# Layer 1 of a two-layer model: smaller pieces of the expert work, deeper buffers, and the expert sum moved to ACT and GpSimd

## The reference

```python
# per batch b (8), T = 512 tokens, C = 128, H = 16 heads of 8
bias attention (a = 0): softmax(q k^T / sqrt(8) + bias[h, j - i]) v, then a gate and a residual
h = affine(layernorm(x));  h = h + causal attention(a = 1) of rmsnorm(h), through Wo
t = rmsnorm(h);  logits = t @ gate_w                          # 8 experts, top 2, gates by softmax
hid = silu(einsum('td,edh->teh', t, w1))                      # 8 experts, 256 wide, all computed
ye = einsum('teh,ehd->ted', hid, w2)
h = h + einsum('te,ted->td', combine, ye);  out = x + gate * h
```

## Time and profile before

| what | us |
|---|---|
| time, median of 3 runs | 2226.02 (2208.1 to 2226.34) |
| time of the profiled execution | 2220.59 |
| its span | 2218.9 |
| busy PE, DVE, ACT, POOL | 1844.8, 1467.2, 1039.1, 807.5 |
| mean granted TensorE clock | 0.923 of full speed |
| first instruction of layer 1 | 778.9 |
| first and last attention tile of layer 1 on DVE | 822.3, 2128.7 |

### The profile page before, as it was taken

One profiled execution on the slowest core, in us unless ns is written; L12 is line 12 of the kernel. 1 busy time (PEld: TensorE's weight loads), 2 busy tenths in 40 slices (PEclk: granted clock), 3 DMA queues, 4 the chain that ended last, 5 costly groups with the idle time before them and its releaser, 6 DMA issues.

```text
span 2218.9 us, 56873 instructions
## 1 busy us (share of the span) xinstructions
PE 1844.8 (83%) x21312; PEld 1333.9 (60%) x21312; DVE 1467.2 (66%) x4551; ACT 1039.1 (47%) x2022; POOL 807.5 (36%) x1180
## 2 busy tenths in 40 slices
PE   3289989898936627998999999999999999999986
PEld 1167767777724415665666666666666666666654
DVE  5477787887720026686776776876876877867754
ACT  2045545544513214555654554654654554654531
POOL 0100110100030035666654654654654654654510
PEclk7589999999968858999999999999999999999988
DMA  3222221211024221112012012012012012011111
GB/s 138 67 84 66 71 63 57 58 51 41 7 81 141 66 83 36 47 35 80 14 67 80 25 67 81 25 64 83 24 62 80 29 62 77 27 62 48 64 37 33
DMA packets 89270, 132.18 MB, mean 60 GB/s; under 512 B 7834, under 2 KB 73754, under 8 KB 87339
## 3 DMA queue, kind: packets, MB, share of 16 engines
q1 hardware_dynamic: 54828, 98.31, 13.3%
q10 hardware_dynamic: 30848, 18.88, 2.9%
q0 software_dynamic: 3328, 11.40, 1.6%
HBM read 98.48 MB, written 30.23 MB: 58 GB/s over the span
## 4 chain that ended last, share of the span: by engine, by line
PE 43%; issue 7%; DVE 5%; DMA 4%; POOL 2%; ACT 2%; SPq 1%; ACTq 0%; POOLq 0%; DVEq 0%
PE ps L1553 14%; PE ps L1566 8%; PE ps L1539 6%; PE ps L1642 5%; PE ps L1636 5%; DMA l_stack<-parts_dram 3%; DVE l_X L1694 2%; PE ps L1576 1%; POOL l_Y L1407 1%; PE ps L1597 1%; ACT PT L1447 1%; DMA parts_dram<-l_parts 1%; PE ps L1586 1%; POOL y L1392 1%; PE ps L1606 1%
## 5 line engine op out<-in xcount | busy, mean ns | idle before, releaser
L1407 POOL TENSOR_SCALAR l_Y<-l_X,l_nmax 128x512 f32<-128x512 f32 (+3 forms) x1024 | 671.2, 657 | 576.4 <-PE ps L1553 327.3
L1447 ACT ACTIVATE PT<-ps 128x512 f32<-128x512 f32 (+3 forms) x1024 | 521.6, 518 | 488.3 <-PE ps L1553 414.1
L1553 PE MATMUL ps<-ident,l_Y 128*128 128x128 f32 x3328 | 563.4, 284 | 56.5 <-POOL l_Y L1407 35.8
L1553 PEld LDWEIGHTS ps<-ident,l_Y 128*128 128x128 f32 x3328 | 389.3, 144 | 263.1 <-issue 136.1
L1694 DVE CUSTOM_DVE_ANT_0 l_X<-ps,strips 128x512 f32<-128x512 f32 x512 | 351.1, 689 | 148.1 <-PE ps L1539 116.6
L1539 PE MATMUL ps<-l_stack 72*128 72x512 bf16 (+3 forms) x1024 | 357.5, 351 | 56.8 <-DVE l_nmax L1694 32.4
L1694 DVE CUSTOM_DVE_ANT_0 l_X<-ps,mask 128x384 f32<-128x384 f32 (+3 forms) x512 | 246.0, 488 | 134.5 <-PE ps L1539 92.2
L1566 PE MATMUL ps<-PT,v_aug 128*32 128x128 f32 x6656 | 236.9, 278 | 0.0
L1566 PEld LDWEIGHTS ps<-PT,v_aug 128*32 128x32 f32 x6656 | 166.9, 110 | 74.6 <-ACT PT L1447 44.8
L1539 PEld LDWEIGHTS ps<-l_stack 72*128 72x128 bf16 x1024 | 105.0, 103 | 89.4 <-DVE l_nmax L1694 46.2
L1642 PE MATMUL ps<-l_w_e,l_hid 128*128 128x128 f32 x1024 | 136.6, 290 | 15.7 <-DVE l_hid L1876 15.7
(11 more groups left out here) (279 smaller groups left out, 2596.3 us busy)
## 6 DMA issues: line engine op xcount, KB each, us to landing
stack<-parts_dram SPq DMA_DIRECT2D x48, 432.0 KB
l_stack<-parts_dram SPq DMA_DIRECT2D x64, 288.0 KB
l_stack<-parts_dram SPq DMA_DIRECT2D x192, 96.0 KB
l_w_e<-in_L_ffn_w_dram ACTq DMA_DIRECT2D x128, 128.0 KB, 2.4
parts_dram<-l_parts SPq DMA_DIRECT2D x32, 384.0 KB, 2.6
strips<-bias_dram POOLq DMA_DIRECT2D x16, 448.0 KB, 11.8
parts_dram<-parts SPq DMA_DIRECT2D x16, 432.0 KB, 2.6
w_e<-in_L_ffn_w_dram SPq DMA_DIRECT2D x16, 256.0 KB, 4.9
```

Of the source, the lines that this page charges most:

```text
L1407: nc.gpsimd.tensor_scalar(Y[:, n % Y_BUFS, 0:w], X[:, n % X_BUFS, 0:w], -1.0, nmax[:, n % 8:n % 8 + 1], ALU.mult, ALU.add).then_inc(y_pool, 1)
L1447: nc.scalar.activation(dst, src, ACT.Exp).then_inc(moved, 1)
L1553: last = nc.tensor.transpose(ps[:, to, k * P:(k + 1) * P], Y[:, n % Y_BUFS, k * P:(k + 1) * P], ident[:])
```

## The change

1. Expert outputs: two halves (`HALVES`) of two token tiles each, in banks 6 and 7. ACT copies each tile from PSUM with its gate as scale into `piece` (which is `xf`), four copies for an expert; GpSimd adds `piece` to `h_tok`, two adds of 128x256. DVE's four additions go.
2. The steps: hidden products two steps apart, output halves two steps apart and later, the whole batch 6 steps earlier in its stage; the last batch has a table of its own (`LAST_STAGES`) with two steps per expert, and its hidden products use banks 0 to 2.
3. Buffers: X 3, Y 4, `hid` 2, expert weights 3. `T_LAG` = 3: a tile is turned, moved and used one step later than before.
4. POOL's gather is issued as one DMA at each of steps 40, 44, 48 and 52.
5. `v_aug` has 10 columns per head in place of 32; bank 5 is cleared once by DVE at the start.

```diff
-MOE_START = {b: TILES * PLACE[1, b + 1] for b in range(B - 2)}
-MOE_START[B - 2] = TILES * PLACE[1, B - 1] + 18
-MOE_START[B - 1] = MOE_START[B - 2] + TILES
-STEPS = MOE_START[B - 1] + TILES
...
-X_BUFS, Y_BUFS, PT_BUFS = 2, 3, 2
-GATHER_AT, PRE_AT, MID_AT, MOE_AT = 40, 2, 17, 1
-MOE_FIRST, MOE_EACH, MOE_F, MOE_YE = 14, 6, 1, 5
-TANH_LAG, MUL_LAG, ADD_LAG = 1, 3, 2
...
+MID_AT = 18
+MOE_START = {b: TILES * PLACE[1, b + 1] - 6 for b in range(B - 2)}
+MOE_START[B - 2] = TILES * PLACE[1, B - 1] + MID_AT + 1
+MOE_START[B - 1] = TILES * len(ORDER) + MID_AT + 1
+HALVES = 2
...
+STAGES = dict(wo=1, add=3, square=4, power=5, scale=7, turn=10, logits=12, read=14, top0=15, top1=16, gap=18,
+              combine=20, first=12, each=6, second=2, tanh=1, mul=2, ye=9, half=2, sum=2)
+LAST_STAGES = dict(wo=0, add=1, square=2, power=3, scale=4, turn=5, logits=7, read=8, top0=10, top1=10, gap=11,
+                   combine=12, first=8, each=2, second=0, tanh=1, mul=1, ye=3, half=0, sum=2)
...
+def hidden_at(b, e, f):
+    p = stages(b)
+    return p["first"] + p["each"] * e + p["second"] * f
...
+def ye_at(b, e, u):
+    p = stages(b)
+    return p["first"] + p["each"] * e + p["ye"] + p["half"] * u
...
+def sum_at(b, e, u):
+    return ye_at(b, e, u) + stages(b)["sum"]
...
+def done_at(b):
+    return sum_at(b, E - 1, HALVES - 1) + 2
...
+X_BUFS, Y_BUFS, PT_BUFS, W_BUFS, VW = 3, 4, 2, 3, HD + 2
+GATHER_AT, PRE_AT = 40, 2
+T_LAG = 3
...
+    return [(b, m - first) for b, first in MOE_START.items() if 0 <= m - first <= done_at(b)]
...
+            slots["T", m - T_LAG] = len(slots)
...
+        piece = xf
...
+        v_aug = [sb(f"v_aug{a}", [P, TT, H, VW]) for a in range(2)]
...
+        hid = sb("l1_hid", [P, 2, FT1, T])
...
+        def side_bank(b):
+            return SIDE if b < B - 1 else 0
+
+        def logits_bank(b):
+            return SIDE2 if b < B - 1 else 1
+
+        def hidden_bank(b, e, f):
+            return SIDE + f if b < B - 1 else (2 + FT1 * e + f) % 3
...
+                def add_up(b, e, u):
+                    h = h_tok[:, b % 3, 2 * u:2 * u + 2, :]
+                    done = (b * E + e) * HALVES + u
+                    pool.wait_ge(ye_read, done + 1)
+                    if e:
+                        pool.wait_ge(ye_added, done - HALVES + 1)
+                    nc.gpsimd.tensor_tensor(h, h, piece[:, 2 * u:2 * u + 2, :], ALU.add).then_inc(ye_added, 1)
...
-                    if pre is not None and pre < B - 1 and i == GATHER_AT:
-                        gather(pre + 1)
+                    if pre is not None and pre < B - 1 and i - GATHER_AT in range(0, 4 * TT, 4):
+                        gather(pre + 1, [(i - GATHER_AT) // 4])
...
+                            for u in range(HALVES):
+                                if k == sum_at(b, e, u) + 1:
+                                    add_up(b, e, u)
...
+                        if i == ye_at(b, e, HALVES - 1) + 1 and n + W_BUFS < B * E:
+                            act.wait_ge(ye_ready, (n + 1) * HALVES)
+                            expert(n + W_BUFS)
...
+                            if i == hidden_at(b, e, f) + p["tanh"]:
+                                act.wait_ge(hid_ready, n * FT1 + f + 1)
+                                if n >= 2:
+                                    act.wait_ge(ye_ready, (n - 1) * HALVES)
+                                nc.scalar.activation(hid[:, e % 2, f, :], ps[:, hidden_bank(b, e, f), :], ACT.Tanh,
+                                                     scale=0.5).then_inc(hid_tanh, 1)
+                        for u in range(HALVES):
+                            if i == sum_at(b, e, u):
+                                act.wait_ge(ye_ready, n * HALVES + u + 1)
+                                if e == 0:
+                                    act.wait_ge(combine_ready, b + 1)
+                                else:
+                                    act.wait_ge(ye_added, (n - 1) * HALVES + u + 1)
+                                for t in (2 * u, 2 * u + 1):
+                                    last = nc.scalar.activation(piece[:, t, :], ps[:, SIDE + u, t * C:(t + 1) * C], ACT.Copy,
+                                                                scale=combine[:, t, e:e + 1])
+                                last.then_inc(ye_read, 1)
...
-                    if i % GROUP == 5 and 1 <= m // GROUP <= 4 * len(ORDER):
+                    if i % GROUP == 6 and 1 <= m // GROUP <= 4 * len(ORDER):
...
+                            last = nc.tensor.matmul(ps[32 * j:32 * j + VW, 5, q * P:(q + 1) * P], v_aug[PLACE[a, b] % 2][:, k, h + j, :],
...
+                    if i == p["wo"]:
+                        if b == B - 1:
+                            pe.wait_ge(shifted, ALL)
+                        elif b:
+                            pe.wait_ge(ye_read, b * E * HALVES)
...
+                                if b == B - 1:
+                                    if e == 0 and f == 0:
+                                        pe.wait_ge(mla_read, b + 1)
+                                    elif e == 1 and f == 0:
+                                        pe.wait_ge(logits_read, b + 1)
+                                    elif e >= 1:
+                                        pe.wait_ge(hid_evac, n * FT1 + f - 2)
+                                elif e == 0:
+                                    pe.wait_ge((mla_read, logits_read)[f], b + 1)
+                                elif e == 1:
+                                    pe.wait_ge(hid_evac, (n - 1) * FT1 + f + 1)
+                                else:
+                                    pe.wait_ge(ye_read, (n - 2) * HALVES + f + 1)
...
+                        for u in range(HALVES):
+                            if i == ye_at(b, e, u):
+                                if u == 0:
+                                    pe.wait_ge(hid_evac, (n + 1) * FT1)
+                                if b == B - 1:
+                                    pe.wait_ge(ye_read, (n - 1) * HALVES + u + 1)
+                                elif e < E - 1:
+                                    pe.wait_ge(hid_evac, (n + 1) * FT1 + u + 1)
+                                else:
+                                    pe.wait_ge(ye_read, (n - 1) * HALVES + u + 1)
+                                for t in (2 * u, 2 * u + 1):
+                                    for f in range(FT1):
+                                        last = nc.tensor.matmul(ps[:, SIDE + u, t * C:(t + 1) * C], hid[:, e % 2, f, t * P:(t + 1) * P],
+                                                                w2_e[:, n % W_BUFS, f, :], start=(f == 0), stop=(f == FT1 - 1))
+                                last.then_inc(ye_ready, 1)
...
+                    if 0 <= m - T_LAG < ALL:
+                        transpose(m - T_LAG)
...
+                    if m % 4 == 1 and 0 <= (m - 9) // 4 < ALL // 4:
+                        values((m - 9) // 4)
...
+                nc.vector.tensor_scalar_mul(ps[:, 5, :], mask[:], 0.0).then_inc(l1_consts, 1)
+                dve.wait_ge(l1_consts, 2)
...
                         dve.wait_ge(rstd_ready[3], b + 1)
+                        if b:
+                            dve.wait_ge(ye_added, b * E * HALVES)
                         nc.vector.tensor_tensor(xf[:], h, bc(rstd[3][:].unsqueeze(2), wide), ALU.mult).then_inc(tok_ready[2], 1)
...
+                        if b:
+                            dve.wait_ge(ye_read, b * E * HALVES)
+                        nc.vector.tensor_scalar_mul(combine[:], small[:, 5], 0.5).then_inc(combine_ready, 1)
...
-                        if i == min(ye_step(e) + ADD_LAG, TILES - 1):
-                            linked()
-                            dve.wait_ge(ye_ready, b * E + e + 1)
-                            if e:
-                                dve.wait_ge(ye_added, b * E + e)
-                            for t in range(TT):
-                                last = nc.vector.scalar_tensor_tensor(out=h[:, t, :], in0=ps[:, SIDE2, t * C:(t + 1) * C],
-                                                                      scalar=combine[:, t, e:e + 1], in1=h[:, t, :],
-                                                                      op0=ALU.mult, op1=ALU.add)
-                            last.then_inc(ye_added, 1)
...
+                    if i % GROUP == 15 and 1 <= m // GROUP <= 4 * len(ORDER):
```

More of the change, by code:

```diff
@@ L1143, in moe_at @@
 def moe_at(m):
-    return next(((b, m - first) for b, first in MOE_START.items() if first <= m < first + TILES), None)
+    return [(b, m - first) for b, first in MOE_START.items() if 0 <= m - first <= done_at(b)]
 def keys(a, q):
@@ L1166, in turned_at @@
         found += [(name, PRE_OF[s]) for at, name in ((10, "xp"), (21, "pq"), (23, "pk"), (25, "pv")) if i == at]
-    moe = moe_at(s * TILES + i)
-    if moe is not None and moe[1] == 10:
-        found.append(("xf", moe[0]))
+    found += [("xf", b) for b, k in moe_at(s * TILES + i) if k == stages(b)["turn"]]
     return found
```

(9 more changed lines are left out.)

145 lines of the change are left out of this document (61 added, 84 removed).

## The result

The changed kernel takes 2155.97 us (median of four runs, 2146.86 to 2173.14) against 2226.18 us before (2208.1 to 2229.0): a ratio of 0.9714, 95% interval 0.964 to 0.9788. The forecast was 2168 us in a range of 2114 to 2208, faster. The profiled execution took 2146.86 us with a span of 2145.1. Of the 73.8 us between the two spans, 8.8 lie ahead of the first attention tile of layer 1 (822.3 us before, 813.5 after), and 7.5 of these in layer 0, which the change doesn't touch. The rest is compared from there on.

The account below looks back on a forecast made before the run. PE was taken to bound layer 1, with stalls on top and a hand-over chain in the tail. Terms -21 - 25 - 8 - 15 + 15 - 2 + 1 = -55 took 2220.6 to 2166, plus 2: 2168 us, range 2114 to 2208.

Parts of the forecast that it names:

- The last batch: Tail after the last attention tile: experts at 3.7 us in place of 5.87; -21 us (-10 to -28).
- The gather: POOL's four indirect DMAs, spread over 12 steps, no longer idle PE: 4 us six times, -25 us (-10 to -32).
- The lag: Layer 1 attention: T_LAG cuts PE's waits for POOL and an extra X helps DVE; -15 us (0 to -50).
- The far end of the range (50): The lag's -50 us, if half of the 93.3 us waits on ACT came from exponentials late for want of Y.
- Where the experts start: Stages 4 to 12: six steps earlier parts picks and mean square on DVE; 1.5 us per stage, -8 (0 to -15).
- What it adds: ACT's copies delay exponentials that free transpose banks; POOL's adds are hidden by slack; +15 us (0 to +40).
- The start of layer 1: Smaller memsets let the gather behind them start 2.3 us sooner; -2 us (0 to -3).
- the values, 0: Narrower values: a unit stays at 128 moving columns, so 0 (down to -10 if weight loads space them).
- (a): Rival: only the tail gains, stage stalls return elsewhere through the two transpose banks; 2198 us, chance 0.20.
- (b): Rival: the lag removes most stalls, those on ACT too; about 50 us more, 2118 us, chance 0.15.
- (c): Rival: slower, the ring of banks 6 and 7 sets the experts' pace in the stages; 2258 us, chance 0.06.
- (d): Rival: POOL's adds are slow, 1.017 us each, and reach PE through Y; +22, 2190 us, chance 0.14.

Follow-up runs that it names:

- The reference: The changed kernel measured once more, nothing altered, beside the follow-up kernels: 2158.67 us, ratio 0.9706 to the kernel before.

## Why the prediction was right, and where it was not

The sum of -55 stands against -66 and -70 in the medians, and its sign and range hold. That it came so near is in part luck: it priced the gather and what the change adds too high and the lag too low, and the reason that it gave for the experts' start was wrong. Term by term:

- **The last batch, -21.** Measured -17.5 and -20.1 in the two profiles of the changed kernel: in the one shown, 16.3 behind the first hidden product and 3.8 before it, where the prediction had 15 and 6. An expert in 3.77 us was forecast at 3.7, by counting PE and ACT. The method (take the ring apart, and go by the busiest engine) is what carried; of the two engines it is PE that has no idle time there.
- **The gather, -25.** The prediction priced it from stages of the kernel before, and there it holds in kind: 3.1 us in each of stages 4 to 10, 17 to 20 in all. But it summed this with the lag as if they were independent. Behind the lag and buffers the split is worth 2 to 10. The weak step is the one that gave the whole 25 to the split: one alone of the two remedies takes most of this stall.
- **The lag, -15.** Too low, by an amount that no run gives cleanly. With the split alone, the stages that hold next to no expert work (0, 2 and the wide ones) take 685.3 us, in the changed kernel 672.3: 13 us for lag, buffers and the later steps. In the masked stages from 4 on it is another 13.5, of which the experts' changes are a part. So lag, start and added work, -8 in the prediction, came to about -26. Undoing the lag alone costs 26 and the buffers 15, but neither leads back to the kernel before, so 41 isn't the size of this term. The prediction took half of the waits that POOL and DVE cause (17 + 13). The runs show that such waits can cost more than their length: with a lag of two the waits on POOL total 12.6 us and the wide stages get 13.4 us more of PE's busy time, half of it by the clock. The far end of the range (50) had another reason, late exponentials, and that one is wrong: the transposes' wait for ACT went only from 93.3 to 87.4.
- **Where the experts start, -8.** Undoing it costs 21 us in the medians, 10 without the long execution and 9 in the profile, for a reason that the prediction didn't see. It looked only at a collision on DVE; the new table ends at step 69, and without the six steps the batch runs over into a wide stage. The collision was only moved: in the changed kernel the picks stand behind the normalising of step 8, and the scores wait there 1.6 us (1286.06 us, above).
- **What it adds, +15.** Leaving the sum out gives 10 us in the medians; by the profile about 9 us in the stages and 8.6 in the tail. The single prices were near (0.368 and 0.739 us); the fifth of ACT's time that was charged to PE was somewhat too much.
- **The experts' weights** had no term, a third buffer seemed safe. Yet it buys no lead: the old table asked for weights six steps ahead of use with two buffers, the new one six steps ahead with three, since an expert holds its buffer longer. The fourth buffer took 11 us out of stages 4 to 10.
- **The start of layer 1, -2, and the values, 0**: 42.1 us up to the first tile of attention in place of 43.4, and 273 ns for a matmul of the values in place of 278.

Of the rivals, (a) is out: the stages gave two thirds of the gain. (b), 2118, is 38 us off; it had the right place (more from the lag) and not the right cause. (c) is out: outputs wait 1.8 us in all for DVE's products. (d) is out: the adds take 0.739 us, not 1.017, and the sum on DVE is 6 us better in the medians, not 22. The reference has a two-input add on DVE too, of 512 columns (812 to 2145 us):

```profile
L1897 DVE TENSOR_TENSOR h_tok<-h_tok,mid_rows 128x512 f32<-128x512 f32 x8 | 5.4, 680 | 0.0
```

DVE takes 0.68 us for 512 columns and GpSimd 0.739 for 256. The Trainium skill's rule (GPSIMD Engine Reference, section 4.1), two-input adds about 2 times slower on GpSimd and so better on VectorE, agrees with these rows: taking half of DVE's 0.68 us for 256 columns, an estimate, the factor is 2.2. The prediction's 2.3 us for two adds, that factor on DVE's old sum of 1.13, is too high all the same, since they take 1.42 us back to back. The run with the sum on DVE has the rule's sign too, but its 6 us can't be told from nothing here.

Of "masked stages near 83, wide ones near 74", 85 to 89 and 75.2 to 76.2 were measured; the masked ones reached 83 to 84 once the fourth weight buffer was in.

## What to carry to other kernels

Price a stall by what follows it too: look at the granted clock and at PE's busy time for the same count of matmuls, since here 70% of the gain of stages 4 to 10 was busy time. When two edits cure one stall, measure each behind the other before adding up their gains, and don't take it as proof when single costs add up. When an edit is undone to price it, undo what moved along with it, or say what stayed. A pipeline's lag and its buffers are one number: keep one buffer more than steps of lag (the two runs with as many buffers as steps were 15 and 29 us slower), and after every change of a schedule count again how many steps ahead of use each load is asked for.

## What the runs showed of the hardware

- A stall of PE can cost beyond its own length, by the lower level of the clock behind it. In stages 4 to 10 nearly the same matmuls (one record in 160 fewer at the last value) took 340.0 us at a mean clock of 0.945, 331.6 at 0.965 and 321.9 at 0.995. It isn't the clock alone: with a lag of two the wide stages had 13.4 us more of PE's busy time, and their clock of 0.988 accounts for 6.5. In four runs of the changed kernel with spans of 2148.8 to 2163.8 us the mean clocks were 0.939 to 0.936, and 0.944 for the 2145.1 us of the first profile: the spread between runs goes with it in sign.
- ACT's copy of 128 columns out of PSUM with a gate from memory takes 0.368 us on average, and four back to back take 1.14. GpSimd's add of 128x256 takes 0.739 on average, and two back to back take 1.42. GpSimd's Y of 512 columns was hardly slower beside it: 0.749 before, 0.759 after.
- A 128 KB weight DMA landed in 2.3 us (median), in up to 9.7, and in 6.1 (median of four) in 20 us in which nine stack DMAs of 96 KB were issued too.
